# Decoder layer with a routed mixture of experts: the order of the first weight loads of the expert stage

## Time and profile before

| what | value |
|---|---|
| median of 3 runs | 1564.33 us (1559.9 to 1565.63) |
| profiled execution, its own time | 1557.66 us |
| its span in the trace | 1556.0 us |
| mean granted TensorE clock | 0.98 of full |
| expert stage in the span | starts at 656.8 us, its 32 turns end at about 1376 us |

### The profile page before, as it was taken

One profiled execution on the slowest core, in us unless ns is written; L12 is line 12 of the kernel. 1 busy time (PEld: TensorE's weight loads), 2 busy tenths in 40 slices (PEclk: granted clock), 3 DMA queues, 4 the chain that ended last, 5 costly groups with the idle time before them and its releaser, 6 DMA issues.

```text
span 1556.0 us, 30312 instructions
## 1 busy us (share of the span) xinstructions
PE 1479.0 (95%) x10344; PEld 1224.5 (79%) x10344; DVE 1129.1 (73%) x2021; ACT 958.8 (62%) x1896; POOL 724.7 (47%) x896
## 2 busy tenths in 40 slices
PE   6999999899999979689999999999999999999998
PEld 4788887778888767478888888888888888876775
DVE  5677665746888788658778777777777777767866
ACT  4566566644566566558777777787777777751211
POOL 2122225232332155346565555656566555446763
PEclk9999999999999989789999999999999999999999
DMA  6012112332221230299777887778777787566664
GB/s 210 1 62 82 51 59 69 100 94 76 62 76 42 72 106 35 80 374 353 267 260 261 285 274 267 262 260 294 268 262 264 274 289 263 170 206 219 192 212 149
DMA packets 116630, 280.25 MB, mean 180 GB/s; under 512 B 17985, under 2 KB 23105, under 8 KB 116545
## 3 DMA queue, kind: packets, MB, share of 16 engines
q1 hardware_dynamic: 98800, 228.25, 43.2%
q0 software_dynamic: 15360, 50.34, 10.1%
q10 hardware_dynamic: 2384, 0.53, 0.2%
HBM read 235.69 MB, written 43.38 MB: 179 GB/s over the span
## 4 chain that ended last, share of the span: by engine, by line
PE 50%; DVE 3%; POOL 2%; DMA 1%; issue 1%; ACT 0%; DVEq 0%; POOLq 0%
PE e_gu L2606 19%; PE e_gu L2608 9%; PE e_dn_rest L2634 6%; PE e_tr L49 3%; PE e_dn_main L41 3%; PE e_dn_main L43 3%; PE e_dn_main L42 3%; POOL h_yk L2816 2%; DVE h_acc L2899 1%; DMA h_yk<-y_dram,h_idx 1%; PE h_gt L41 1%; PE h_gt L42 1%; PE h_gt L43 1%; PE h_up L43 1%; PE h_up L42 1%
## 5 line engine op out<-in xcount | busy, mean ns | idle before, releaser
L2369 POOL TENSOR_TENSOR e_hid<-e_h_raw,e_hid 128x128 fp32r<-128x128 f32 (+1 forms) x192 | 166.5, 868 | 221.8 <-ACT e_hid L2434 221.8
L2606 PE MATMUL e_gu<-e_xT_hi_lo,e_wg 128*128 128x384 f32 (+1 forms) x768 | 231.7, 358 | 0.7 <-issue 0.7
L2606 PE MATMUL e_gu<-e_xT_hi_lo,e_wu 128*128 128x384 f32 (+1 forms) x768 | 230.6, 356 | 0.0
L2608 PE MATMUL e_gu<-e_xT_hi_lo,e_wu 128*128 128x192 f32 (+1 forms) x768 | 193.5, 252 | 0.0
L2608 PE MATMUL e_gu<-e_xT_hi_lo,e_wg 128*128 128x192 f32 (+1 forms) x768 | 193.3, 252 | 0.0
L2377 POOL TENSOR_TENSOR e_wd<-e_raw_d,e_wd 96x512 fp32r<-96x512 f32 x64 | 131.7, 2058 | 35.8 <-ACT e_wd L2419 35.8
L2606 PEld LDWEIGHTS e_gu<-e_xT_hi_lo,e_wg 128*128 128x128 f32 (+1 forms) x768 | 138.1, 180 | 6.4 <-issue 2.0
L2512 DVE TENSOR_TENSOR e_total<-e_gu,e_low 128x384 f32<-128x384 f32 (+1 forms) x192 | 105.5, 549 | 51.6 <-ACT e_low L2429 51.6
L2429 ACT ACTIVATE e_low<-e_gu 128x384 f32<-128x384 f32 (+1 forms) x192 | 93.2, 485 | 80.1 <-PE e_gu L2608 78.0
L2608 PEld LDWEIGHTS e_gu<-e_xT_hi_lo,e_wg 128*128 128x128 f32 (+1 forms) x768 | 140.1, 182 | 1.4
L2606 PEld LDWEIGHTS e_gu<-e_xT_hi_lo,e_wu 128*128 128x128 f32 (+1 forms) x768 | 138.0, 180 | 3.8
(11 more groups left out here) (425 smaller groups left out, 3965.2 us busy)
## 6 DMA issues: line engine op xcount, KB each, us to landing
e_raw_g<-in_L_ffn_Wg_dram SPq DMA_DIRECT2D x64, 704.0 KB, 4.4
e_raw_u<-in_L_ffn_Wu_dram SPq DMA_DIRECT2D x64, 704.0 KB
e_raw_d<-in_L_ffn_Wd_dram SPq DMA_DIRECT2D x64, 512.0 KB, 6.0
y_dram<-e_y_main SPq DMA_DIRECT2D x64, 256.0 KB, 6.4
e_raw_d<-in_L_ffn_Wd_dram SPq DMA_DIRECT2D x64, 192.0 KB, 6.9
y_dram<-e_y_rest SPq DMA_DIRECT2D x64, 128.0 KB, 7.2
s_xr<-in_x_dram SPq DMA_DIRECT2D x16, 256.0 KB, 3.9
x_dram<-s_x SPq DMA_DIRECT2D x16, 256.0 KB, 2.5
```

The lines of the kernel that those rows point to most:

```text
L2369: pool.tensor_tensor(hid[b][1][0:n, c, :], h_raw[g.odd][b][0:n, c, 0:P], hid[b][0][0:n, c, :].bitcast(F32), ALU.subtract).then_inc(s_hl, 1)
L2606: pe.matmul(bank[0:n, 0:2 * CAP], w[b][0][:, k, m:m + n], xT[:, :, k, toks], start=k == 0, stop=False)
L2608: ins = pe.matmul(bank[0:n, 0:CAP], w[b][1][:, k, m:m + n], xT[:, 0, k, toks], start=False, stop=k == KC - 1)
```

## The change

Four edits, all at the start of the expert stage:

1. SyncE loads gate and up of the first expert, then waits until all three gathers of the first turn have landed, and only then loads gate and up of the second expert. Both down weights of the first turn come behind these, then gate and up of expert 0 of the second turn.
2. The shared expert's loads and `load_xf` move behind `turn(pair(0))`, that is behind gate and up of expert 1 and both down weights of the second turn, and ahead of the loop.
3. In the first turn the gathers take their indices from `names` itself, so the copies to `idx` are gone there.
4. The copies of later turns count on their semaphore from one lower.

```diff
--- before.py
+++ after.py
@@ -2301,21 +2301,14 @@
                     sp.dma_start(y_out[bass.ds((2 * g.n + b) * CAP + P, REST), :], y_rest[b * REST:(b + 1) * REST, :]
                                  ).then_inc(s_str, 16)
 
+            load_gu(pair(0), 0, True)
+            for j in range(COLS):
+                sp.wait_ge(s_x[j], 16)
+            load_gu(pair(0), 1, True)
             for b in range(2):
-                load_gu(pair(0), b, True)
                 load_d(pair(0), b, True)
             load_gu(pair(1), 0, False)
 
-            s_gate, s_up, s_down = shared_in
-            for src, dst in ((s_gate, shared_raw[0][:, :, 0:MS]), (s_up[:, 0:FULL * P], shared_raw[1][:]),
-                             (s_up[:, FULL * P:MS], shared_raw[0][:, :, MS:MS + HALF])):
-                sp.dma_start(dst, src.rearrange("(k p) m -> p k m", p=P)).then_inc(shared_loaded, 16)
-            for c in range(FULL):
-                sp.dma_start(shared_raw[2][:, c, :], s_down[c * P:(c + 1) * P, :]).then_inc(shared_loaded, 16)
-            for r in (0, HALF):
-                sp.dma_start(shared_raw[2][r:r + HALF, FULL, :], s_down[FULL * P:MS, :]).then_inc(shared_loaded, 16)
-
-            ahead.load_xf(sp, 0)
 
             def turn(g, first, last):
 
@@ -2333,6 +2326,16 @@
                     store_rest(g.last())
 
             turn(pair(0), True, False)
+            s_gate, s_up, s_down = shared_in
+            for src, dst in ((s_gate, shared_raw[0][:, :, 0:MS]), (s_up[:, 0:FULL * P], shared_raw[1][:]),
+                             (s_up[:, FULL * P:MS], shared_raw[0][:, :, MS:MS + HALF])):
+                sp.dma_start(dst, src.rearrange("(k p) m -> p k m", p=P)).then_inc(shared_loaded, 16)
+            for c in range(FULL):
+                sp.dma_start(shared_raw[2][:, c, :], s_down[c * P:(c + 1) * P, :]).then_inc(shared_loaded, 16)
+            for r in (0, HALF):
+                sp.dma_start(shared_raw[2][r:r + HALF, FULL, :], s_down[FULL * P:MS, :]).then_inc(shared_loaded, 16)
+
+            ahead.load_xf(sp, 0)
             with sp.Fori(0, (turns - 2) // 2) as i:
                 for g in two_pairs(i):
                     turn(g, False, False)
@@ -2345,17 +2348,18 @@
             def gather(g, part):
                 j0, j1 = idx_parts[part]
                 n = g.n
+                ids = names
                 if not (isinstance(n, int) and n == 0):
-
+                    ids = idx
                     pool.wait_ge(s_t, COLS * (n - 1) + j1)
-                pool.tensor_copy(idx[:, j0:j1], names[:, bass.ds(n * COLS + j0, j1 - j0)]).then_inc(s_idx[part], 1)
-                pool.wait_ge(s_idx[part], n + 1)
+                    pool.tensor_copy(idx[:, j0:j1], names[:, bass.ds(n * COLS + j0, j1 - j0)]).then_inc(s_idx[part], 1)
+                    pool.wait_ge(s_idx[part], n)
                 if not isinstance(n, int):
 
                     pool.tensor_tensor(carry[:], xones[:], xones[:], ALU.mult)
                 for j in range(j0, j1):
                     pool.indirect_dma_start(out=xg[:, j * H:(j + 1) * H], out_offset=None, in_=xf,
-                                            in_offset=bass.IndirectOffsetOnAxis(ap=idx[:, j:j + 1], axis=0)
+                                            in_offset=bass.IndirectOffsetOnAxis(ap=ids[:, j:j + 1], axis=0)
                                             ).then_inc(s_x[j], 16)
 
             def hidden_lo(g, b):
```

## The result

The changed kernel takes 1573.23 us, the median of 20 runs (1559.77 to 1581.14), beside 1568.73 us for the kernel before (1559.90 to 1573.75, 20 runs). The ratio is 1.004, with an interval of 1.0023 to 1.0056: **slower by 6.3 us, within 3.6 to 8.8** (the two medians are 4.5 us apart, inside the same interval). The profiled execution took 1579.45 us with a span of 1577.7. That is 21.7 us more than the span before, and most of it is not by the change: the expert stage starts 4.5 us later in this span, its last turn is 1.6 us longer because the granted clock fell to 0.50 for about 3 us there (four of the fourteen traces of this case show that), and the stage behind the loop is nearly 10 us longer.

What follows compares the result with a forecast made beforehand. TensorE was taken to bound the loop turns, 21.8 us each. The third turn starting 3.2 us later plus 1.7 us of low clock made 4.9 us slower; put on 1561.9 us, the forecast was 1566.8 us, range 1560 to 1573.

Steps and rivals of the forecast that it cites:

- Index copies: First turn on GpSimd: first gather up to 0.5 us sooner, third gather issued at 661.5 instead of 662.06.
- Length of a gather with a short queue: First turn's gathers: 4.0 us each, between bounds of 3.2 and 7.3, so the third lands at 665.5.
- the third rival: First turn: gathers not quicker, taking 7.3 us whatever stands in the other queue; 8.2 us slower; chance 0.12.
- Front: First gate_up: token halves done at 667.98 instead of 670.36, a gain of 2.4 us.
- Restart of the queue: Loads behind SyncE's wait: full rate only at 666.8, so transfers fall behind by 1.0 MB or 2.7 us.
- The second turn's gate weights: Needed at 682.2, landing at 680 with 4.4 MB ahead of and with them; covered by 2 us, no cost.
- The fourth turn's gathers: Start about 701.5 instead of 708.66, moving 0.52 MB beside the third turn's gate weights; cost 1.4 us.
- Landing of the third turn's gate weights: Expert 0 of the third turn: weights land at 711.3 instead of 707.18; TensorE starts that turn 3.2 us later.
- The clock: Third turn: after TensorE stands 5.6 us the clock falls, costing 1.7 us, with both ends 0 and 1.7 kept.
- The shared loads moved back: Behind the second turn's loads: frees ScalarE's hidden 4.37 us, gives TensorE nothing; same loads stand ahead of the third turn's gate weights.
- The rival that the front's gain would stand: Third turn's weights are not late, so TensorE keeps 2.4 us: faster by 2.4, 1559.5 us; chance 0.18.
- The rival without a fall of the clock: Third turn: all as forecast without the 1.7 us of low clock; 3.2 us slower, 1565.1 us; chance 0.25.

Runs made afterwards that it cites:

- held back: Changed kernel, with GpSimd holding the fourth turn's first two gathers until the third turn's weights have landed; ratio 1.0024 to the kernel before.
- the filled gap: Changed kernel with 80 transposes of the identity on TensorE ahead of the third turn, where it stood waiting; ratio 1.0024 to the kernel before.
- one load left in place: Kernel before with shared loads and indices as changed, no SyncE wait, old first-load order, first shared load in its old place; ratio 1.0016.
- the move alone: Changed kernel without the SyncE wait and with first loads in their old order; shared loads and indices stay as changed; ratio 1.0052 to the kernel before.
- the wait alone: Changed kernel with the shared loads put back in their old place; wait and gathers' indices stay as changed; ratio 1.0037 to the kernel before.
- the shared loads are spread: Changed kernel with shared loads and first tokens spread behind the loads of later turns, SyncE wait kept; ratios 0.9974 and 0.9964 to the kernel before.

## Why the prediction was right in its mechanism and wrong in its number

The forecast was 1566.8 us in a range of 1560 to 1573, and the measured median is 1573.23, 0.2 above it. The step that failed is the anchor, the time of the kernel before to which the difference was added: "The four executions average 1561.9, and I put the forecast on that". Twenty runs put the kernel before at 1568.73, 6.8 above my anchor and 4.4 above the median that I was shown. The predicted difference, 4.9 us slower, lies inside the measured 3.6 to 8.8, and the chance of 0.82 for a change within 0.5% went to what happened. In four comparisons the kernel before had medians of 1566.6, 1559.8, 1567.5 and 1559.3, so its level moves by 8 us from one to the next. In the traces the expert stage starts between 653.6 and 661.5 us in the span, and what follows its loop takes 177 to 193 us. A range for an absolute time has to hold that scatter; mine held the cases of the difference.

By its steps:

- *Index copies.* I took the third gather 0.56 us sooner. It was 0.2 (5.05 against 5.24 us from the first load), since the first gather, without its copy, is issued only 0.04 us sooner (2.24 against 2.28).
- *Length of a gather with a short queue.* Taken 4.0 us, measured: the third was issued at 666.36 and SyncE went on at 670.09, 3.7 us. Right, and the third rival fell with it.
- *Front.* Predicted 2.4 us, got 3.1 to the start of the first gate_up, since the up weights landed 0.5 us sooner, which I had held fixed. The clock also came back earlier in that gate_up, so TensorE was 4.0 us ahead at the second one (682.04 against 681.53, from first loads at 661.31 and 656.82). All of it only made the later gap longer, as predicted for the 2.4. The gap is 8.3 us instead of 5.6 because TensorE reaches it 2.3 us sooner than I had it (713.3 - 661.3 = 52.0 us, forecast 711.1 - 656.8 = 54.3) and leaves it 0.4 later.
- *Restart of the queue.* Predicted 1.0 MB or 2.7 us behind. Measured 1.0 MB at 12 us. It then grew to 1.4 MB by 22 us, in the stretch at 340 instead of 377 GB/s, which I had not foreseen, and was still 1.3 MB at 45: 3.7 us at 357 GB/s, for 2.7 predicted.
- *The second turn's gate weights.* I had them land at 680 - 656.8 = 23.2 us, with 2 us to spare. ScalarE waited 0.39 us for them, until 24.3. My 4.4 MB held the weights alone and not the second turn's three gathers, 0.8 MB, which are issued 9.9 us after the first load. TensorE didn't wait for it.
- *The fourth turn's gathers.* Taken 1.4 us; about 0.9 when held back, with the scatter said there.
- *Landing of the third turn's gate weights.* Predicted 711.3 - 656.8 = 54.5 us from the first load; measured 54.9. That these agree so well is in part luck: the backlog was 1.0 us more than predicted and the gathers some 0.5 less, and two further traces with the same start have 56.3 and 56.7. The third turn starts 3.7 us later than before, for 3.2 predicted.
- *The clock.* Predicted 1.7, measured 2.3 by the filled gap (2.6 to 2.9 in three other kernels), as the clock stayed low for 4.4 us of the turn and not 3.6. Of the two ends kept, a fall was the right one. The rule of the Trainium skill, "TensorE: Matmul & The Clock Gate", section "HAM oscillation — how this bites in real kernels", holds here: a stop for transfers is followed by matmuls at the low clock. This trace agrees, at 0.50 for 4.4 us behind a gap of 8.3; and the gap of 1.4 us with one load left in place left the clock at 1.00, with a first matmul of 0.43 us instead of 0.68.
- *The shared loads moved back.* Priced at nothing of its own, "exactly the same loads stand ahead of it". For the changed kernel the sum came out right only because the wait had already pushed the transfers back: the hole between 22 and 27 us is closed by what is late. Alone, the move costs 9.7 us at the mark and the wait 7.2; together 5.9. The bytes agree: 27 us from the first load the move alone is 2.0 MB behind the kernel before, the wait alone 1.5 and both together 1.3. The 1.3 us between the wait alone and both is within the scatter of the marks, and the run times, 1.0052, 1.0037 and 1.0040, have intervals that overlap and don't order the three. The two edits share one idle time, and I had not seen that the shared loads were the queue's filling.

The rival that the front's gain would stand is out in the changed kernel; a gain of that kind is seen when the shared loads are spread. The rival without a fall of the clock is out.

## What to carry to other kernels

When loads are reordered, don't only count the bytes ahead of the critical one: go through the queue in time and ask for each stretch whether anything in it may be issued. A large load with no deadline, placed before an issue that waits for a buffer, is what kept the engines at 397 GB/s here; moved behind it, the same bytes come on top of a hole. And before making a load wait for a gather, look where the slack ends first: here it was 0.9 us two turns later, and of the orders that were run only the one that spread the shared loads, a part in each of several turns, turned the front's gain into time.

## What the runs showed that I had not expected

With the move alone a queue that was nearly empty for 5 us made the weights 7.6 us late (58.0 against 50.4 us from the first load). The bytes moved account for it. At 27 us this kernel had moved 7.7 MB and the one before 9.8, which is 5.7 us at 362 GB/s: 1.6 MB of the 2.0 are the hole; most of the rest was lost just before 22 us, when the queue was already running out. And by the time that the weights were there it had moved 18.8 MB and the one before 18.1, another 1.9 us, with the fourth turn's two gathers (0.5 MB) among what went beside the critical load.

In all kernels with a wait on SyncE the stretch from 12 to 22 us ran at 328 to 356 GB/s, with a DMA share of 1.01 in the changed kernel, against 377 at 1.02 before: busy engines that move less. Down weights and gathers fall together there, but no run took one of them away, so the cause stays open. And removing the two copies on GpSimd, 0.4 us of work, moved the first gather by 0.02 us.
